# Local attention in a fused block: one folded, once-transposed row of probabilities, and a value ring shifted by a token

## The reference

```python
h = shift_token(x)                      # half of the channels come from the token before
q, k, v = split(h @ wqkv); q, k = rotary_xpos(l2norm(q) * qs, l2norm(k) * ks)
# queries of window w see the keys of window w-1 ("older") and of window w ("newer"):
mask = (i < j) | (i > j + WINDOW) | (j == -1)
attn = softmax(where(mask, -max, q @ k.T))     # 128 queries x 256 keys
x = x + (attn @ v) @ wo
h = layernorm(shift_token(x)); x = x + (a * gelu(g)) @ w2 + b2      # a, g = halves of h @ w1 + b1
```

## Time and profile before

| | |
|---|---|
| median of 3 runs | 3470.91 us (3468.52 to 3475.22) |
| the profiled execution | 3477.93 us, span of its instructions 3475.8 us |
| PE / DVE / ACT / POOL busy over the span | 96% / 68% / 61% / 61% |
| granted TensorE clock, mean | 0.986 of 2.4 GHz |
| phase L | from about 665 us to the end |

### The profile page before, as it was taken

How to read it: one execution, slowest core, us unless ns; L and a number is a source line. 1 busy time by engine, 2 the same in 40 slices (tenths; PEclk the granted TensorE clock), 3 DMA queues, 4 the chain that set the end, 5 groups by cost and what they waited for, 6 DMA issues and landing times.

```text
span 3475.8 us, 80515 instructions
## 1 busy us (share of the span) xinstructions
PE 3334.4 (96%) x24412; PEld 2587.4 (74%) x24412; DVE 2361.7 (68%) x7850; ACT 2129.8 (61%) x5246; POOL 2109.6 (61%) x2124
## 2 busy tenths in 40 slices
PE   3999999799999999999999999999999999999998
PEld 1666666477777777878787788887878787877777
DVE  2999999656666666666666666666666666666664
ACT  1555555356666666666666666666666666666665
POOL 0888888655555555555555555666666666666664
PEclk7999999899999999999999999999999999999999
DMA  6111111100000000000000001111111111111110
GB/s 206 61 45 43 45 44 44 33 19 23 22 23 22 23 22 23 22 23 22 23 22 23 22 23 35 35 35 35 35 35 36 34 36 35 35 35 35 35 35 29
DMA packets 152911, 124.74 MB, mean 36 GB/s; under 512 B 22564, under 2 KB 148888, under 8 KB 152224
## 3 DMA queue, kind: packets, MB, share of 16 engines
q1 hardware_dynamic: 146352, 110.67, 10.5%
q10 hardware_dynamic: 6128, 8.86, 0.8%
HBM read 77.44 MB, written 42.02 MB: 34 GB/s over the span
## 4 chain that ended last, share of the span: by engine, by line
PE 79%; DVE 9%; issue 7%; POOL 2%; ACTq 1%; DMA 1%; DVEq 0%; ACT 0%; SPq 0%; POOLq 0%
PE bank L534 25%; PE bank L708 18%; PE bank L541 12%; PE bank L716 10%; PE bank L688 7%; PE bank L668 7%; DVE shared L1017 2%; DVE a_den L1006 1%; ACTq L745 1%; DVE z L972 1%; DVE a_den L1004 1%; DVE a_moments L1037 1%; DVE a_moments L961 1%; DVE shared L998 1%; DVE gated L1032 1%
## 5 line engine op out<-in xcount | busy, mean ns | idle before, releaser
L1263 POOL TENSOR_TENSOR shared<-shared,share_of 128x512 f32<-128x512 f32 x512 | 522.0, 1040 | 1012.0 <-DVE share_of L1115 1012.0
L534 PE MATMUL bank<-WQKV,xT 128*128 128x512 f32 x1536 | 705.9, 596 | 1.0 <-ACT xT L731 1.0
L708 PEld LDWEIGHTS bank<-zT,W 128*128 128x128 f32 x5632 | 648.9, 192 | 61.0 <-issue 59.8
L731 ACT ACTIVATE shared<-bank 128x512 f32<-128x512 f32 (+1 forms) x640 | 347.9, 554 | 516.4 <-PE bank L541 378.8
L708 PE MATMUL bank<-zT,W 128*128 128x128 f32 x5632 | 649.6, 275 | 0.9 <-ACT zT L885 0.9
L865 ACT ACTIVATE shared<-shared,negmax 128x256 f32<-128x256 f32 x1024 | 505.9, 496 | 1.6
L534 PEld LDWEIGHTS bank<-WQKV,xT 128*128 128x128 f32 x1536 | 283.3, 191 | 256.0 <-issue 247.7
L1250 POOL TENSOR_TENSOR rnorm<-clamped,HALF 128x8 f32<-128x8 f32 x256 | 420.3, 1642 | 77.2 <-DVE clamped L1088 72.5
L1106 DVE CUSTOM_DVE_ANT_0 shared<-bank,MASK 128x256 f32<-128x256 f32 x1024 | 375.6, 421 | 73.6 <-issue 73.5
L1103 DVE MEMSET spare<- 128x1 f32 x512 | 30.2, 59 | 417.6 <-PE bank L668 412.6
L541 PEld LDWEIGHTS bank<-IDENT,shared 128*128 128x128 f32 x2176 | 249.5, 142 | 82.6 <-DVE shared L1011 64.7
(11 more groups left out here) (132 smaller groups left out, 6150.0 us busy)
## 6 DMA issues: line engine op xcount, KB each, us to landing
X<-xl_rows SPq DMA_DIRECT2D x128, 128.0 KB, 2.3
X<-in_x SPq DMA_DIRECT2D x64, 128.0 KB, 2.1
x_tiles<-ax SPq DMA_DIRECT2D x64, 128.0 KB, 1.7
xl_rows<-axl SPq DMA_DIRECT2D x64, 128.0 KB, 1.7
XS<-xl_rows SPq DMA_DIRECT2D x128, 64.0 KB, 2.1
xm_rows<-X SPq DMA_DIRECT2D x128, 64.0 KB, 1.6
xs<-xm_rows SPq DMA_DIRECT2D x128, 64.0 KB, 1.8
xl_rows<-X SPq DMA_DIRECT2D x64, 128.0 KB, 1.7
```

The lines of the kernel that those rows point to most:

```text
L534: mm = nc.tensor.matmul(held(tile, key)[:, 0:cols], lhsT[c], rhs[c], start=(c == 0), stop=(c == len(lhsT) - 1))
L708: mm = nc.tensor.matmul(held(tile, key)[:, k * P:(k + 1) * P], W1[:, tile.l, c, at:at + P], zT[:, c], start=(c == 0), stop=(c == KC - 1))
L731: return nc.scalar.activation(dst, src, ACT.Copy)
L1263: G.tensor_tensor(probs, probs, share_of[:, h:h + 3:2].unsqueeze(2).to_broadcast((P, 2, 2 * WINDOW)), ALU.mult).then_inc(done[f"share{b}"], 1)
```

## The change

The newer and the older probabilities of a query never need the same column: older key j counts for queries i <= j, newer key j for i >= j. So older probability j is added to column j+1 of the newer half (`fold0..3`, new, on POOL), and one 128-column row holds both, but for older key 127, which stays in its own column. `share` scales these 129 columns only, and `turn_p0/1` transpose 4 blocks each, 8 a tile instead of 16. `keep_p0/1` (now both on DVE) make two matrices out of each transposed one by multiplying it with a triangular mask: `pTnew` (CAUSAL) and `pTold` (the new mask LATER). A row r of `pTold` now belongs to older key r-1, so `weigh` multiplies it by values that are shifted by one token; row 0 (older key 127) is brought by SP's new step `first_key0/1`, four DMAs each that move a column of 128 single elements into a row. SP's new step `move_v` makes the shifted older values after the last `weigh` of a tile: 127 rows of 2 KB from `vring[.., 0]` to `vring[.., 1]`, one partition down, and the last row to partition 0. `keep_v` always writes `vring[.., 0]`, and `weigh` and `keep_v` wait for `move_v` of the stream's tile before (4 slots back). `max` waits until the columns of the tile before are read (`moved_first`). All lists and banks are new.

```diff
-        MASK = sb("MASK", [P, 4, WINDOW])
+        MASK = sb("MASK", [P, 5, WINDOW])
+        LATER = sb("LATER", [P, P])
...
-        pT = [carve(2048 + 512 * b, 4, P) for b in range(PAIRS)]
+        pTold, pTnew = ([carve(2048 + 1024 * k + 512 * g, 4, P) for g in range(2)] for k in range(2))
...
+        moved_v, moved_first = [sem(f"moved_v_{q}") for q in range(STREAMS)], [sem(f"moved_first_{g}") for g in range(2)]
...
+        def old_values(eng, tile):
+
+            if tile.least >= STREAMS:
+                eng.wait_ge(moved_v[tile.seq], tile.at.block * 64 + 32 * (USES * tile.l + tile.s // STREAMS))
...
+            def first_key(g, tile):
+
+                after(sp, done[f"keep_p{g}"], tile, per=2, ahead=-1)
+                for k in range(4):
+                    column = shared[:, (4 * g + k) * 2 * WINDOW + P - 1:(4 * g + k) * 2 * WINDOW + P]
+                    with nc.allow_non_contiguous_dma(reason="a column to a row"):
+                        sp.dma_start(pTold[g][0:1, k], column).then_inc(moved_first[g], 16)
+
+            def move_v(tile):
+
+                after(sp, done[latest(ORDER_L["PE"], WEIGH)], tile)
+                sp.dma_start(vring[tile.seq][1:P, 1], vring[tile.seq][0:P - 1, 0]).then_inc(moved_v[tile.seq], 16)
+                sp.dma_start(vring[tile.seq][0:1, 1], vring[tile.seq][P - 1:P, 0]).then_inc(moved_v[tile.seq], 16)
...
+                        keys = kring[tile.seq][rows, 2 * g + k]
+                        if tile.s < STREAMS:
+                            keys = keys[:, ::-1]
                         mm = nc.tensor.matmul(held(tile, f"sim{2 * g + e}")[:, k * 2 * WINDOW:(k + 1) * 2 * WINDOW], qT[rows, 2 * g + k],
-                                              kring[tile.seq][rows, 2 * g + k].rearrange("p o t -> p (o t)"),
-                                              start=True, stop=True)
+                                              keys, start=True, stop=True)
...
-            def turn_p(p, tile):
-                after(pe, done[f"share{p}"], tile)
-                turn(tile, f"p{p}", [pr[p][:, k] for k in range(4)]).then_inc(filled[f"p{p}"], 1)
+            def turn_p(g, tile):
+                for b in (2 * g, 2 * g + 1):
+                    after(pe, done[f"share{b}"], tile, per=3)
+                turn(tile, f"p{g}", [pr[b][:, 2 * k + 1] for b in (2 * g, 2 * g + 1) for k in range(2)]).then_inc(filled[f"p{g}"], 1)
 
             def weigh(p, tile):
 
 
-                after(pe, done[f"keep_p{p}"], tile)
+                g = p // 2
+                after(pe, done[f"keep_p{g}"], tile, per=2)
                 after(pe, done["keep_v"], tile)
+                after(pe, moved_first[g], tile, per=64)
+                old_values(pe, tile)
                 first = f"weigh{p}" == earliest(ORDER_L["PE"], WEIGH)
                 if first:
                     claim(pe, tile, "o")
-                for kb in range(2):
+                for kb, pT in enumerate((pTnew, pTold)):
                     for k, h in enumerate(heads_of(p)):
                         mm = nc.tensor.matmul(held(tile, "o")[k * LD:(k + 1) * LD, p * P:(p + 1) * P], vring[tile.seq][:, kb, h * LD:(h + 1) * LD],
-                                              pT[p][:, 2 * k + kb], start=(first and kb == 0), stop=(kb == 1), skip_group_check=True)
+                                              pT[g][:, 2 * (p % 2) + k], start=(first and kb == 0), stop=(kb == 1), skip_group_check=True)
...
-                after(act, done[last_weigh], tile, back=STREAMS)
+                old_values(act, tile)
                 if tile.least < STREAMS:
                     act.wait_ge(done["a_mod"], ALL)
-                copy(vring[tile.seq][:, tile.s // STREAMS], held(tile, "v")[:]).then_inc(done["keep_v"], 1)
+                copy(vring[tile.seq][:, 0], held(tile, "v")[:]).then_inc(done["keep_v"], 1)
...
-            def keep_p(b, tile):
-                after(act, filled[f"p{b}"], tile)
-                after(act, done[f"weigh{b}"], tile, back=1)
-                first_use(act, tile)
-                copy(flat(pT[b]), held(tile, f"p{b}")[:]).then_inc(done[f"keep_p{b}"], 1)
...
+            V.tensor_scalar(LATER[:], CAUSAL[:], -1.0, 1.0, ALU.mult, ALU.add).then_inc(gate_step, 1)
...
-                after(dve, filled[f"p{b}"], tile, back=1)
+                after(dve, filled[f"p{b // 2}"], tile, back=1)
+                after(dve, moved_first[b // 2], tile, back=1, per=64)
...
-                now = MASK[:, 1:3] if tile.s < STREAMS else MASK[:, 0:2]
+                now = MASK[:, 2:4] if tile.s < STREAMS else MASK[:, 0:2]
...
+                V.reciprocal(share_of[:, h:h + 3:2], den[:, h:h + 3:2]).then_inc(done[f"share{b}"], 1)
+
+            def keep_p(g, tile):
+                after(dve, filled[f"p{g}"], tile)
+                for p in (2 * g, 2 * g + 1):
+                    after(dve, done[f"weigh{p}"], tile, back=1)
+                got = held(tile, f"p{g}").rearrange("p (a t) -> p a t", a=4)
                 first_use(dve, tile)
-                V.tensor_copy(pT[b].rearrange("p a t -> p (a t)"), held(tile, f"p{b}")[:]).then_inc(done[f"keep_p{b}"], 1)
+                for pT, mask in ((pTold, LATER), (pTnew, CAUSAL)):
+                    V.tensor_tensor(pT[g], got, mask[:].unsqueeze(1).to_broadcast((P, 4, P)), ALU.mult).then_inc(done[f"keep_p{g}"], 1)
...
+            def fold(b, tile):
+                after(pool, done[f"exp{b}"], tile)
+                probs = pr[b].rearrange("p (e b) t -> p e (b t)", e=2)
+                G.tensor_tensor(probs[:, :, P + 1:2 * P], probs[:, :, P + 1:2 * P], probs[:, :, 0:P - 1], ALU.add).then_inc(done[f"share{b}"], 1)
+
             def share(b, tile):
-                after(pool, done[f"invert{b}"], tile)
+                after(pool, done[f"share{b}"], tile, per=3, ahead=-1)
                 h = heads_of(b)[0]
-                probs = pr[b].rearrange("p (e b) t -> p e (b t)", e=2)
-                G.tensor_tensor(probs, probs, share_of[:, h:h + 3:2].unsqueeze(2).to_broadcast((P, 2, 2 * WINDOW)), ALU.mult).then_inc(done[f"share{b}"], 1)
+                probs = pr[b].rearrange("p (e b) t -> p e (b t)", e=2)[:, :, P - 1:2 * P]
+                G.tensor_tensor(probs, probs, share_of[:, h:h + 3:2].unsqueeze(2).to_broadcast((P, 2, P + 1)), ALU.mult).then_inc(done[f"share{b}"], 1)
```

More of the change, by code:

```diff
@@ L63 @@
 ORDER_L = {
[L64 to L76, removed]
+    "SP": [(0, "load"), (3, "shift"), (3, "late"), (2, "first_key0"), (2, "first_key1"), (4, "store"), (2, "move_v")],
+    "PE": [(3, "project_o"), (1, "project_v"), (1, "turn_q"), (2, "turn_p0"), (1, "turn_k"), (0, "turn_x"), (2, "turn_p1"),
+           (4, "narrow"), (1, "score0"), (0, "project_k"), (1, "score1"), (2, "weigh0"), (2, "weigh1"), (2, "weigh3"),
+           (2, "weigh2"), (3, "turn_z"), (0, "project_q"), (3, "widen0"), (3, "widen1"), (3, "widen2")],
+    "ACT": [(1, "keep_v"), (1, "keep_q"), (0, "keep_x"), (1, "keep_k"), (0, "square_k"), (1, "exp0"), (1, "exp1"),
+           (2, "keep_o"), (3, "affine"), (0, "square_q"), (1, "exp2"), (1, "exp3"), (3, "gelu")],
[4 rows of a table added]
+           (3, "root_x"), (4, "finish"), (3, "add_b2"), (0, "root_k"), (0, "add_k"), (0, "scale_k"), (1, "fold0"),
+           (0, "root_q"), (0, "scale_q")],
 }
@@ L522, in store @@
                 sp.dma_start(dst, X[tile.s][:]).then_inc(stored[tile.seq], 16)
-            run_tiles(sp, "L", ORDER_L["SP"], {"load": load_tile, "late": late, "shift": shift, "store": store}, SEGMENTS_L)
+            run_tiles(sp, "L", ORDER_L["SP"], {"load": load_tile, "late": late, "shift": shift, "store": store, "move_v": move_v,
+                                             **{f"first_key{g}": partial(first_key, g) for g in range(2)}}, SEGMENTS_L)
             for q in range(STREAMS):
                 sp.wait_ge(stored[q], 16 * USES * (DEPTH + 1))
+                sp.wait_ge(moved_v[q], 32 * USES * DEPTH)
         @block.tensor
@@ L722, in _ @@
             steps.update({f"score{g}": partial(score, g) for g in range(2)})
-            steps.update({f"turn_p{p}": partial(turn_p, p) for p in range(PAIRS)})
+            steps.update({f"turn_p{g}": partial(turn_p, g) for g in range(2)})
             steps.update({f"weigh{p}": partial(weigh, p) for p in range(PAIRS)})
@@ L768, in _ @@
             load(MASK[:, 0:2].rearrange("p b t -> p (b t)"), window[:, 4 * WINDOW:6 * WINDOW])
-            load(MASK[:, 3], window[:, 0:WINDOW])
+            load(MASK[:, 3], window[:, 4 * WINDOW + WINDOW:6 * WINDOW])
+            load(MASK[:, 4], window[:, 0:WINDOW])
             assert count[0] == LAYER_LOADS
@@ L907, in _ @@
             steps.update({f"exp{b}": partial(probs, b) for b in range(PAIRS)})
-            steps.update({f"keep_p{b}": partial(keep_p, b) for b in (0, 2)})
             run_tiles(act, "L", ORDER_L["ACT"], steps, SEGMENTS_L)
@@ L1169, in _ @@
             steps.update({f"invert{b}": partial(invert, b) for b in range(PAIRS)})
```

(3 more changed lines are left out.)

22 lines of the change are left out of this document (9 added, 13 removed), and 15 rows, old and new, of tables (BANK_L, FILLS, ORDER_L).

## The result

The changed kernel takes 3848.23 us, the median of 4 runs (3841.84 to 3849.72), beside 3472.42 (3468.52 to 3475.22, 4 runs) for the kernel before: the ratio is 1.108, with a 95% interval of 1.106 to 1.1099. It is slower, as forecast; but 3545 was predicted, and 3848 lies outside the range that ended at 3640. The predicted mechanism is in the trace. What was wrong is its size. The granted TensorE clock is 0.969 on average (0.986 before); it isn't the cause, since PE's pieces keep their lengths, `narrow` 2.59 us in both.

The account below looks back on a forecast made before the run. PE was taken as the bound, at 21.41 us a slot. +0.52 us x 124 full slots = +64, plus 10 for filling and draining, on 3477.9 profiled: 3551.9, or 3545 us in the runs' terms; range 3365 to 3640.

Parts of the forecast that it names:

- the wait for X: Before `turn_x`, PE waits 1.4 us in every slot for X, loaded behind the 127-row copy; a slot becomes 21.9 us.
- the 13.0 us until X is there: From the last `weigh`: 0.2 until SP knows, 1.4 DMA without data, 10.9 copy, 0.5 load's data on that engine.
- the 8.9 us from `turn_x` to the last `weigh`: PE's remaining work in the loop after X arrives, 8.9 us, added to 13.0 for a slot of 21.9 us.
- The columns, left to a rival: Second layer: shift's write held by the copy, last columns at 21.4 us, `weigh3` at 21.0: +25 us; within a 10% rival.
- One engine, and load behind it: `move_v`: 127 is prime, so equal shares put the copy on one DMA engine; the next `load` is served behind it.
- the main case: One-engine copy above 10.2 to 10.4 us makes PE wait for X: slower, 54% for 3480 to 3640 us.
- +10 for filling and draining: Outside full slots, uncovered column DMAs and a pipeline one slot deeper cost some 10 us, estimated from three such delays.
- The fast case: Copy short or not in the way (18%), or spread over 16 engines (10%): slot 20.53 us, kernel 3372 us.
- folds 724 ns and `keep_p` 690: POOL's folds were forecast near 0.73 us each, DVE's `keep_p` multiplications near 0.69 us.
- no wait for POOL before `turn_p0`: Rival, 2%: POOL comes late before `turn_p0`, needing 8.9 us, or 10.4 at 1.04 apiece, where PE needs 8.8.
- SP's ten extra DMAs: Ten DMAs more a slot, 0.58 us apart, 5.8 us of a mostly idle queue; the columns hidden by 1.6 us or more.
- X was to take 10 us or more from issue to landing: Expected sign of the load held behind the copy: X and XS both take 10 us or more from issue to landing.

Follow-up runs that it names:

- spread version: The changed kernel with the 127-row copy issued as two copies, of 112 and 15 rows: 3520.38 us, ratio 1.0123 to the kernel before.
- the best version here: The spread version with LATE loads behind the column DMAs, `project_k` ahead of both scores, and ScalarE's and VectorE's lists reordered: 3421.83 us, ratio 0.984.
- the version with 113 rows: The changed kernel with the 127-row copy issued as two copies, of 113 and 14 rows: 3707.15 us, ratio 1.0669 to the kernel before.

## Why the prediction was right in kind and wrong in size

The prediction added 0.52 us to a slot and 10 us at the ends. Measured were 2.24 us in the first layer, 3.02 in the second and 28.5 at the end. The step that failed is the wait for X: both terms of its sum were too small, the 13.0 us until X is there (14.2) and the 8.9 us from `turn_x` to the last `weigh` (9.4). The columns, left to a rival, and the ends make up the rest.

- **One engine, and load behind it: right.** The equal shares read from packet counts held; 112 and 15 rows against 113 and 14 show it.
- **How long X takes: off, the term that failed first.** Predicted was X 13.0 us after the last `weigh`, with 10.9 for the copy. PE's L715 ends its piece at 1510.65 and `turn_x` starts at 1524.89: 14.2, and the median is 14.2 in both layers. By the packets of this slot the copy takes 11.8 of it (1512.00 to 1523.77), the load's rows behind it 0.55 (0.5 was said), and what lies before the first row and behind the last 1.35 and 0.53, together 1.9 where 1.6 was said. The pace of a full stretch was right (24.6 GB/s measured, 23.9 from the earlier trace rows), but the copy begins slowly, 14 rows in a stretch of 2 us where later 24 go through. The 1.2 us more are, over 127 slots, 152 us.
- **PE's part of the loop: off, the second term.** The prediction let 8.9 us lead from `turn_x` to the last `weigh`. It is 9.4 in the median slot of the first layer and 9.6 in the slot shown (1501.03 to 1510.65), where `weigh` takes 2.11 instead of 1.92. Most of the 0.5 is that the durations came from pieces of before that stood in another order: `score0` and `score1` adjacent 1.93, now 2.12 on either side of `project_k`, which takes 1.91 instead of 1.72; together 0.38. Moving them together again in the experiments shows both sizes.
- **The two terms together.** 14.2 + 9.4 is 23.6 where 21.9 was said. The prediction's wait was a difference of two near sums (13.0 - 11.6 = 1.4), so errors of 1.2 and some 0.5 turned a loss of 0.5 us a slot into one of 2.2.
- **The columns: hidden in most of the first layer, the rival's size wrong in the second.** The prediction had the chain add_o, `xm_rows` held by the copy, LATE, columns, `weigh3` as a rival worth +25 us, and left it out of the sum. It became true beside the main case: 63 slots at 24.44 instead of 23.66 are +49 us. From the last `weigh` to `turn_x` a slot takes 14.2 us in both layers; from `turn_x` to the end of the last `weigh` it takes 9.4 in the first and 10.1 in the second (medians), so the whole difference lies there. The list of waits names only 18.8 us of it. The last column lands 22.9 us after the last `weigh` in the slot of the second layer below (2824.50 to 2847.41), where 21.4 was said:

```profile
2831.80 1.74 PE bank L555 x8
2833.56 0.43 DVE X L1151
...
2834.16 4.72 DMA xm_rows<-X
...
2839.56 0.33 SPq L508
...
2844.99 2.42 DMA shared<-shared
...
2847.65 1.11 PE bank L715 x16
```

- **"+10 for filling and draining": too small.** From the last `turn_x` to the end the kernel before takes 66.2 us and the changed one 94.7: +28.5. In the spread version, whose full slot equals that of before, the end (+22.6) and the first slots of the loop rounds (+20) are all of the 43 us. The first slots of the rounds had no term in the sum.
- **The fast case: wrong as well.** The rivals in which the copy is not in the way had a slot of 20.53 us. That was right only where the order lets PE work alone. In the changed order two more things stand in the way: ScalarE's list (0.36 us of `project_q`'s piece and 0.11 of `widen`'s, gone with `exp0` first) and the scores apart (0.39). The prediction summed ScalarE's work and found it free; it did not follow the list from `project_k` to `widen`. With the copy spread the kernel takes 3520 us and not 3372.
- **Right:** folds 724 ns and `keep_p` 690, no wait for POOL before `turn_p0` in full slots, and eight of SP's ten extra DMAs cost a full slot nothing once the copy is spread (21.41 us with and without them). Shares take 619 ns, less than the bound of 0.73 us.
- **Not as said:** X was to take 10 us or more from issue to landing. XS takes 8.4 and X by the page 2.2. `load` is issued 3.6 us later than in the tiles where SP is not held in L532, so less of the copy is left. That does not change when XS lands, 14.2 us after the last `weigh` also in the tiles where SP isn't held. And X is not there after 2.2 us: its last rows go at 1523.79 to 1524.13, 8.3 us after its issue (1515.86). X and XS count on one semaphore, on which the page reads the landing; so go by the packets, or by the later of the two.
- **A small slip in the sum:** its terms, 13.0 + 8.9 - 21.41, make 0.50 us a slot and not 0.52, 2 us in all.

The account of 3845.3 - 3475.8 = 369.5 us, from the starts of `turn_x`: the first layer's 64 slots +151.3, the second's 63 +188.2, the end +28.5, before the first +1.5. Split by the medians (an estimate): 127 slots at +2.24 are 284; the columns in the second layer are 47 more; the other slots of the first layer, those at the start of a loop round above all, 8. The prediction's sum had 74 in all.

## What to carry to other kernels

Count the rows of a copy before its bytes. Here the copies of 127 and of 113 rows, which no number from 2 to 16 divides, went to one DMA engine; the 128-row transfers behind it, on the same queue or another, had a share on that engine. Splitting off 15 rows gave back 328 us. Ask then where in the loop the copy starts and what is needed soonest behind it: the same copy was worth 0.25% where the next load was issued long enough ahead, and moving it past one transfer only made the next one late. Where two chains of a loop are within a us of each other, sum both with the new neighbours of each instruction, and walk each engine's list through the loop rather than add up its work: the best version here (3421.83 us) came from such reorderings on top of the spread copy.

## What the runs showed of the hardware that was not expected

- While one DMA engine works through 127 rows, SP is in most tiles held in issuing the next DMA: 3.9 to 4.4 us for the one-row copy where issues elsewhere take mostly 0.33 to 0.7, and 0.55 to 0.57 in 17 of the 128 tiles. In the version with 113 rows it is 2.1 to 3.4 us for the copy of 14, and 0.9 in 17 tiles. In the kernel before with the copy added, the hold falls on the load (3.09 and 3.87 us in two slots). Why, and what sets the length, was not tried; the landing of XS didn't depend on it.
- A copy on one engine begins slowly: the first 30 rows take 3.7 us, later ones 0.083 us each, in every tile. Why is open.
- A transfer on another queue waits for the engine too: `xm_rows` lands after 4.6 us instead of 1.6.
- TensorE: `project_k` takes 1.91 us behind a score (matmuls of 64 rows) and 1.72 behind `narrow`; two scores apart take 2.12, together 1.93. That the change between 64 and 128 rows is the cause fits the orders run, but `weigh` behind a score keeps 1.90, so it isn't settled.
- The first slot of a loop round: PE waits for nothing that the list of waits names, in one such slot of the spread version 2.0 us ahead of `project_o` (1703.79) and 1.86 within it. The slot is 23.6 to 25.1 us in the first layer before, 25.6 to 28.7 in the spread version. The columns' part was measured (above). In the spread version there are 18 such gaps, 34.3 us in all, and in each a packet of queue q8, whose kind the page gives as `instruction`, starts 0.7 to 1.1 us ahead of the gap. For the one at 1703.79 (1702 to 1704):

```profile
q8 instruction: 1, 0.02, 3.7%
```

So PE may be waiting for its next instructions there. No run tests it, and why these slots are longer after the change than before stays open.
